# A decoder's first stage: the written orders of four engines replaced by others

## Time and profile before

| | |
|---|---|
| Runs of the kernel | 4591.91, 4595.98, 4602.75 us, median 4595.98 |
| Profiled execution, its time | 4600.57 us |
| Profiled execution, its span | 4598.8 us (1.8 us lie around it) |
| Mean granted clock of TensorE over the span | 0.967 |
| Instructions | 149905, of them TensorE 61616 matmuls and as many weight loads |

### The profile page before, as it was taken

One profiled execution on the slowest core, in us unless ns is written; L12 is line 12 of the kernel. 1 busy time (PEld: TensorE's weight loads), 2 busy tenths in 40 slices (PEclk: granted clock), 3 DMA queues, 4 the chain that ended last, 5 costly groups with the idle time before them and its releaser, 6 DMA issues.

```text
span 4598.8 us, 149905 instructions
## 1 busy us (share of the span) xinstructions
PE 4426.6 (96%) x61616; PEld 3422.3 (74%) x61616; DVE 3567.7 (78%) x11101; ACT 3495.8 (76%) x9695; POOL 2653.1 (58%) x2208
## 2 busy tenths in 40 slices
PE   7999989999999999999999999999999779999999
PEld 5777667777777777777777777777777568888888
DVE  4666599888888888888888888888888556666675
ACT  3555488888888888888888888888888546766776
POOL 3444377777676676766667666777667323333332
PEclk9898799999999999999999999999999869999999
DMA  3000000000000000000000000000000100000000
GB/s 97 4 4 4 3 2 2 2 2 2 25 2 2 2 25 2 2 2 2 25 2 2 2 25 2 2 2 6 4 6 7 45 1 4 4 4 4 4 4 6
DMA packets 40195, 40.16 MB, mean 9 GB/s; under 512 B 4164, under 2 KB 37976, under 8 KB 38744
## 3 DMA queue, kind: packets, MB, share of 16 engines
q1 hardware_dynamic: 39512, 30.59, 2.2%
HBM read 28.48 MB, written 2.10 MB: 7 GB/s over the span
## 4 chain that ended last, share of the span: by engine, by line
PE 89%; DVE 6%; ACT 3%; issue 1%; POOL 0%; SPq 0%; DMA 0%; ACTq 0%; DVEq 0%; POOLq 0%
PE ps L532 73%; PE ps L536 16%; ACT BIG L885 2%; DVE BIG L1086 2%; DVE sm L1097 1%; DVE BIG L1094 1%; ACT L885 1%; DVE BIG L1091 1%; POOL BIG L1523 0%; ACT BIG L877 0%; DVE sm L1094 0%; POOL sm L1526 0%; DVE BIG L1164 0%; DVE sm L1090 0%; DVE sm L1193 0%
## 5 line engine op out<-in xcount | busy, mean ns | idle before, releaser
L877 ACT ACTIVATE BIG<-ps 128x512 f32<-128x512 f32 (+6 forms) x3216 | 1480.7, 505 | 608.5 <-PE ps L536 441.5
L532 PE MATMUL ps<-WB,BIG 128*128 128x128 f32 (+1 forms) x8576 | 1896.6, 363 | 7.8 <-DVE BIG L1086 5.5
L1523 POOL TENSOR_TENSOR BIG<-BIG,sm 128x1024 f32<-128x1024 f32 (+1 forms) x864 | 1223.2, 1425 | 745.5 <-DVE sm L1094 503.3
L532 PEld LDWEIGHTS ps<-WB,BIG 128*128 128x128 f32 x8576 | 1152.8, 192 | 410.2 <-issue 378.2
L532 PEld LDWEIGHTS ps<-BIG 64*64 64x64 f32 (+2 forms) x37888 | 944.0, 131 | 294.2 <-issue 193.7
L1523 POOL TENSOR_TENSOR BIG<-BIG 128x512 f32<-128x512 f32 x768 | 974.2, 1276 | 323.5 <-DVE BIG L1086 322.7
L532 PE MATMUL ps<-BIG 64*64 64x64 f32 (+4 forms) x37888 | 1071.2, 225 | 24.1 <-DVE BIG L1164 8.4
L1097 DVE TENSOR_REDUCE sm<-BIG 128x8 f32<-128x512 f32 (+3 forms) x1472 | 872.7, 617 | 140.0 <-ACT BIG L885 133.1
L536 PE MATMUL ps<-t_ident,BIG 128*128 128x128 f32 x6016 | 873.7, 282 | 94.1 <-DVE BIG L1094 42.2
L536 PEld LDWEIGHTS ps<-t_ident,BIG 128*128 128x128 f32 x6016 | 707.7, 144 | 253.9 <-issue 108.2
L885 ACT ACTIVATE BIG<-ps,sm 128x64 f32<-128x64 f32 (+1 forms) x3104 | 678.5, 330 | 103.4 <-DVE sm L1097 100.8
(11 more groups left out here) (121 smaller groups left out, 3054.3 us busy)
## 6 DMA issues: line engine op xcount, KB each, us to landing
WB<-in_Wqkv SPq DMA_DIRECT2D x6, 1536.0 KB, 7.5
y_sb<-in_ctx SPq DMA_DIRECT2D x16, 256.0 KB, 2.9
WB<-in_Wo SPq DMA_DIRECT2D x6, 512.0 KB, 8.9
x_sb<-in_x SPq DMA_DIRECT2D x8, 256.0 KB, 5.4
WB<-in_F_W SPq DMA_DIRECT2D x1, 2048.0 KB, 8.6
WB<-in_F_W SPq DMA_DIRECT2D x8, 256.0 KB, 6.2
out<-x_sb SPq DMA_DIRECT2D x8, 256.0 KB, 2.3
WB<-in_W SPq DMA_DIRECT2D x6, 341.0 KB
```

The source lines that it names most:

```text
L532: return te.matmul(o, l, r, start=start, stop=stop, skip_group_check=not check)
L877: return se.activation(o, i, ACT.Copy)
L1523: return pe_.tensor_tensor(o, a, b, op)
```

## The change

The four strings of `AB_ORDER` are replaced, and the loops over passes run to `len(AB) + 9` instead of 8, since offsets now reach 9. What a phase does, buffers, waits and the sum of instructions stay.

```diff
--- before.py
+++ after.py
@@ -76,11 +76,11 @@
 
 
 AB_ORDER = {
-    "pe": "J1 b12 V3 s4 O3 a22 u5 b22 T1 o3 a32 w3 t5 G1 b32 D1 p14 a42 v4 x3 b42 X0 q3 Z2 y5 a11 W2 p04",
-    "act": "e07 v7 Z5 q6 a14 W5 J3 j3 p07 O5 a24 o5 T3 e16 a34 t7 D3 C3 a44 x5 p16 X2",
-    "dve": "n6 m05 w4 st24 st0 ag24 ep24 d33 t33 m2 xn24 q2 e2 d43 ag0 t02 ep0 y6 xn0 ss1 d12 b1 U3 be1 t12 R1 s14 "
-           "so3 Q1 s23 K1 s04 m14 N3 d22 r5 t22",
-    "pool": "u08 pw27 l5 pw3 rn4 ro6 u17",
+    "pe": "v5 a33 w4 G2 t6 b33 D2 p15 a43 x4 y6 b43 X1 q4 Z3 p05 a12 W3 J1 b12 V3 s4 O3 a22 u5 b22 T1 o3",
+    "act": "O7 a26 T5 o7 v8 a36 e18 D5 C5 t9 a46 x7 e08 p18 X4 Z6 q7 a15 W6 J4 j4 p08",
+    "dve": "d15 be4 t15 s17 R4 Q4 so6 s26 K4 m17 s07 N6 d25 r8 t25 m07 n8 w6 ag1 st26 ag26 ep26 d35 t35 xn26 m4 q4 e4 "
+           "y8 d45 xn2 t04 ep1 ss3 b3 st0 U5",
+    "pool": "pw1 u16 u06 pw25 l3 rn2 ro4",
 }
 
 DE_ORDER = {
@@ -276,7 +276,7 @@
         uC1 = {(u.at["l"], u.at["t"]): u for u in CC if u and u.kind == "C1"}
         uC2 = {(u.at["l"], u.at["g"]): u for u in CC if u and u.kind == "C2"}
         DE = ring_units([("DE", dict(t=t)) for t in range(NT)] if "D" in stages else [], "de", 8)
-        SLOTS_AB, SLOTS_C, SLOTS_DE = len(AB) + 8, len(CC) + 7, len(DE) + 8
+        SLOTS_AB, SLOTS_C, SLOTS_DE = len(AB) + 9, len(CC) + 7, len(DE) + 8
 
         def unit(seq, n):
             return seq[n] if 0 <= n < len(seq) else None
@@ -382,7 +382,7 @@
             full, turn = [()] * 8, 0
             for u in seq:
                 u.bank, u.after = {}, {}
-            for n in range(len(seq) + 8 if seq else 0):
+            for n in range(len(seq) + 9 if seq else 0):
                 for u, ph in phases(order, seq, "pe", n):
                     if ph not in emptied:
                         u.after[ph] = ()
```

## The result

The changed kernel takes 4617.39 us (median of 5 runs, 4616.01 to 4630.99) against 4595.98 for the kernel before (5 runs, 4591.91 to 4618.25): ratio 1.0051, 95% interval 1.0034 to 1.0068. It is **slower** by 21 us. The profiled execution took 4627.69 us, span 4625.9, mean clock 0.961.

The account below looks back on a forecast made before the run. A chain of waits through three engines, 14.00 us a full-clock slot, plus 2.6 us per clock fall bounds it. 5.8 + 8.7 - 2 = +12.5 on the profiled 4600.57 gives 4613, 4608 against the median; range 4566 to 4628.

Parts of the forecast that it names:

- `st`, +0.20: VectorE, `ss` to `t2`: moving `st` in delays `a3` from 5.66 to 5.86 us after `ss`; bounds 0 and 0.3.
- `v` fills the gap: TensorE before `a3`: `v`, 0.32 us, goes where TensorE idles 0.27 us; costs nothing, 0.15 us of the gap stays.
- `a3` to `Z`, 5.24: TensorE's second piece: 5.14 us less 0.32 for `v` plus 0.42 for `y`; bounds 5.1 and 5.25.
- `Z` to `ss` stays: Third piece stays 3.20 us: TensorE reaches `J` about 0.4 us sooner but wins nothing, ScalarE being busy throughout.
- +0.25 us a slot, 5.8 us in all: Steady part: each of 23 full-clock slots lengthens by 0.25 us, at most 0.3, from 14.00; in all +5.8 us.
- 3.3 more falls, 8.7 us: Steady part: longer slots bring 3.3 more clock falls at 2.6 us, +8.7 us; bounds 0 and +20, eight more falls.
- One full slot for every two low ones: Steady part: slots lengthened by 0.25 us have this share, instead of 11 full to 12 low.
- Filling and draining, -2 us: Before and after the steady part: `y` out of the way of `J` gives back about 0.4 us in five slots.
- What would show it: Signs in the steady part: full slots 14.2 to 14.3 us, `a3` at 5.86, 0.1 to 0.2 us idle, clock 0.86 to 0.88.
- Rival (1): Steady part: `v` ahead of `a3` holds the clock, twelve falls become four or so, -15 us, to -35; chance 0.27.
- Rival (2): Slot: VectorE no longer holds up `a3`, `Z` comes sooner, slot nears 13.52 us; -11 us, to -30; chance 0.10.
- Rival (3): Whole change: nothing measurable, one gap shrinks, another grows, falls stay as many; within 5 us; chance 0.08.

Follow-up runs that it names:

- b_st: Kernel before with only VectorE's `st` moved into the stretch between `ss` and `U`; ratio 1.0038.
- a_st: Changed kernel with VectorE's `st` and `ag` put back where they were before; ratio 1.0024 to the kernel before.
- b_vt: Kernel before with TensorE's `v` moved between `o` and `a3`, ScalarE's copy of it moved along, and `t` put behind `G`; ratio 0.9994.
- b_v: Kernel before with `v` alone moved: on TensorE between `o` and `a3`, on ScalarE its copy behind `T`; ratio 1.0059.
- b_r_U_m: Kernel before with VectorE's `U` directly behind `ss`, `r` and `m1` behind `t2`, and ScalarE's `e1` behind `a3`; ratio 1.0026.
- b_st_y: Kernel before with only VectorE's `st` moved between `ss` and `U` and TensorE's `y` moved before `b4`; ratio 1.0076.
- a_y: Changed kernel with `y` put back behind `Z` on TensorE and behind `t0` on VectorE; ratio 1.0081 to the kernel before.
- b_y: Kernel before with TensorE's `y` alone moved from behind `Z` to before `b4`; ratio 1.0038.
- b_vt_r_U: Kernel before with `v` ahead of `a3`, its ScalarE copy moved along, `t` behind `G`, VectorE's `r` behind `t2` and `U` directly behind `ss`; ratio 0.9987.

## Why the prediction was right, and where not

The forecast was slower, 4608 us, own range 4599 to 4624; it took 4617, inside it. The way and the mechanism hold: a longer slot, and more falls because of it. Against its own profiled execution the sum of +12.5 us stands beside +27.1 measured (+21 between the medians). By its steps:

- **`st`, +0.20: right for `st`**, b_st has 5.84. That the changed kernel has 5.85 to 5.86, as forecast, is two further errors that cancel. The other moves, priced at 0 for this piece, cost 0.1 us (`t2` at 5.34 in a_st), so `t2` comes at 5.54 and not at 5.45. And `a3` starts 0.06 us behind the transpose's end for 0.15.
- **`v` fills the gap: right**, with sizes off. The forecast left 0.1 to 0.2 us of idle time before `a3` and priced `v` at 0; there is no idle time, and `v` in it gives back 0.09 us (b_vt has `a3` at 5.55 for 5.65). `a3` is still released by the transpose.
- **`a3` to `Z`, 5.24: measured 5.29 (a_st), by errors that cancel.** `y` costs 0.13 and not 0.42; `v` saves 0.17 and not 0.32, and `t` behind `G`, priced at 0, costs 0.16 (b_v 4.96, b_vt 5.12).
- **`Z` to `ss` stays: right**, 3.19 for 3.20. TensorE comes to `J` sooner (1.58 us before `ss` for 1.27) and gains nothing, as ScalarE sets the end.
- **+0.25 us a slot, 5.8 us in all: slightly small.** The full slot would be 14.33, that is +0.33. Over 23 slots that is 7.6 us. Another 2.6 us are small stalls of TensorE inside a step ahead of `a3`, beyond those that the kernel before has (4.7 for 2.1 us, against each kernel's usual `ss` to `a3`); the forecast had none.
- **3.3 more falls, 8.7 us: this term was mis-sized.** Eleven more came (23 for 12), beyond its bound of eight. The steady part's 36.1 us less 7.6 and 2.6 leave 25.9 for them, about what ten cost at 2.6 us; the eleventh was cut short, in a slot of 15.46 us. "One full slot for every two low ones" is just what b_st (14.18), a_st (14.13) and b_r_U_m (14.21) show. But the low slot that came is of 16.91 us, not 16.85, and with it no full slot is left. The earlier trace rows had pairs of low slots in three cases of six between 16.80 and 17.06 us; so few cases allowed every share up to all of them, and the bound of eight, which left three full slots standing, had no row behind it. The profiled execution also shows the loss somewhat large: its low time is 362 us in the whole kernel, the mean of the five executions 346, and 300 before. At 2.6 us for a fall of 6.8 us, those 46 us of low time are 17 to 18 of the 26 us between the mean times.
- **Filling and draining, -2 us: too small**, -10.1 measured. The reason given, `y` out of the way of `J`, is not what the rows show: the draining part has a clock of 0.78 for 0.67 in the earlier trace rows, some 21 us less low time, which at 2.6 us for 6.8 is 8 us. a_st has the same short draining (71.9 us) while b_st_y, with `st` and `y` alone, has 73.8 and a filling of 125.4. Single profiles differ by several us here as well (draining 79.3 and 76.9 in the two of before), so no one edit is shown as the cause of the better clock.
- **What would show it:** a steady clock of 0.86 to 0.88 was forecast; it is 0.80, with no full slot at all. Of the signs for the pieces, `a3` at 5.86 and `Z` to `ss` at 3.20 came; the idle time at `a3` did not. The two signs named as refuting it (0.92 or more; a full slot of 13.9 or less) did not come.

**Rival (1), the clock falls less often with `v` ahead of `a3`: fell.** Its premise was half right. In b_vt and its kin falls are fewer (7 to 9), but they last 10 to 12.5 us, and in a_y they last 9.2; b_v has 8.9; in all kernels with `v` or `y` between `a4` and `b4` they last 6.8 to 7.6. So such a product decides how soon the clock comes back more than whether it falls. That reading rests on five kernels against eight, in single profiles, b_v with its own wait and b_vt by its slowest execution among the five. In the change `y` takes `v`'s old place, so that nothing of this is seen. The Trainium skill ("TensorE: Matmul & The Clock Gate", "Part 4: PE-mode transpose") has a real matmul count for more than a transpose; `v` right behind the transposes T and o brought no gain that can be measured in any run here. Nor are the transposes what stands last ahead of a fall: in the kernel before, every fall begins behind the start of `a3`. **Rival (2)** fell as well: `a3` is released by VectorE's transpose in the changed kernel too, and the full slot of a_st is 14.13, not on the way to 13.52. **Rival (3)** is refuted by the interval, 1.0034 to 1.0068.

**Why length counts so much.** Among the kernels with a product between `a4` and `b4`, ordered by full slot: 13.91, 13.98, 13.98 us have 11, 12, 10 falls; 14.13, 14.18, 14.21 have 17, 17, 17; 14.33 (worked out) and b_st_y's 5.84 + 5.27 + 3.18 = 14.29 have 23. b_y fits less well, 20 falls with 14.19 (14.09 by its usual pieces). That the numbers of falls stand so neatly in rows is in part luck, as two profiles of one kernel differ by two. The low time of all executions gives the same order more coarsely: 286 to 303 us for full slots up to 13.98, 320 to 345 for 14.13 to 14.21, 346 and 366 for the two longest. Where in the slot the clock falls hardly changes: all 22 falls in the two profiles of before begin 0.1 to 0.8 us behind the start of `a3`, and 21 of the 23 after the change between 0.02 us ahead of it and 0.55 behind. So the change did not move the fall, it made it come in more slots. The relation was measured; what in the chip makes it was not. The loss comes in steps of 2.6 us out of changes of 0.1 us. **Open:** why b_y and a_y fall more often than their length says, why the draining part keeps more of the clock, and why the changed order has more stalls inside TensorE's steps. No version tried beats the kernel before by more than can be measured: the best is b_vt_r_U, 0.9987 (0.9974 to 1.0000).

## What to carry over

Where the clock falls in some repeats of a cycle and not in others, don't price an edit by its own microseconds: look how often each length of the cycle is followed by a fall, each length by itself, and let the range reach to a fall in every cycle. Compare a profile's granted clock with that of the other executions before you count its falls. Put small instructions of an engine behind the one that the cycle waits for, not ahead of it; 0.2 us of `st` cost 0.38% of the whole kernel (0.20 to 0.56). When a phase is moved in an order that hands out PSUM in a ring, see first whose bank each later phase now gets.

## What was not expected of the hardware

- The clock falls 7 to 23 times in 23 cycles, by the kernel, though TensorE is busy 16.53 of 16.91 us in the usual low slot after the change, and its longest pause in that kernel's steady part is 0.78 us. A fall lasts 6.8 us in most cases, and up to 17.1 in b_v and b_vt.
- A product of two instructions placed elsewhere in a cycle of 14 us goes with another length of a fall: 6.8 to 7.6 us on average with `v` or `y` between `a4` and `b4`, 8.9 to 12.5 without.
- TensorE starts later behind its releaser when it has idled. `a3` begins 0.15 us after the end of VectorE's transpose when there is idle time ahead of it, 0.05 to 0.06 us after it when another product stands right ahead.
- TensorE can stop in the middle of a step with no semaphore to wait for. In the slot from 361.29, TensorE's timeline of the kernel after:

```profile
367.35 0.39 PE L532 MATMUL ps<-BIG 32*32 32x32 f32 x24
368.40 0.26 PE L532 MATMUL ps<-BIG 32*32 32x32 f32 x8 [0.66 <-issue]
```

  Its `b2` takes 1.24 us instead of 0.39 from start to the next phase. Such stalls explain the slots of 17.4 to 17.6 us. After the change the steady part has six, at 163.6, 232.2, 300.0, 368.4, 436.6 and 504.8 us, of 0.50 to 0.78 us: one in every fourth slot. The profile of the kernel before has four of over 0.15 us, of 0.16 to 0.66. All that the DMA queues carry between 361 and 370 us is `q8 instruction: 2, 0.03`, two transfers of instructions; whether the stall is a wait for one of them, no run shows.
